# A scan layer with a hand-written slot order: residual products through another PSUM bank, the preparation six slots later

## The chip, the cores and the metric

The kernel runs on one core of one Trainium2 chip. The metric is the device time of one execution in microseconds, as the median of several runs. The core has a TensorE (PE), a VectorE (DVE), a ScalarE (ACT) and a GpSimd (POOL); SyncE (SP) issues most of the transfers. Each engine works off its own list of instructions in order, and waits on semaphores for the others.

## The reference

The input x is 2 sequences of 4096 tokens with 256 features. The first layer is a selective scan (the reference calls it attention), the second a mixture of 16 experts. Each is wrapped in `x + layernorm(layer(layernorm(x)))`. The change touches the first layer only:

```python
xn = _rmsnorm(x, rms_w)
xs, res = jnp.split(xn @ W_in, 2, axis=-1)          # 512 and 512 channels
xs = silu(causal_depthwise_conv(xs, conv_w) + conv_b)
dt, Bm, Cm = split(xs @ W_x)                        # 512, 16, 16
dt = softplus(dt @ W_dt)
A_disc = exp(-exp(A_log) * dt[..., None])
Bx = dt[..., None] * Bm[:, :, None, :] * xs[..., None]
# per channel and state, over the tokens: h = A_disc * h + Bx; y = sum over the 16 states of h * C
y = y * silu(res)
return residual + y @ W_out
```

## The kernel before

**Tiles and steps.** The tokens are cut into 16 tiles of 512, the two sequences in turn. Step i scans tile i. It is divided into 64 slots: slot t holds scan t, which runs 128 of the 8192 pairs of a channel and a state over the 512 tokens of the tile. `all_steps` (L246) writes out the steps; two steps form the body of a hardware loop, the first two and the last ones stand outside. Four scans in a row are a quad, 16 quads a tile.

**What a scan needs.** ACT makes its decay, exp(a * dt), in one of three PSUM banks `pa` (L678), two slots ahead; DVE scans (L822) with the input bq. The input product of a quad (`rep` times `B`) is made for even quads, and for quads 13 and 15, by DVE (L808), for the odd quads 1 to 11 by POOL (L930). After a quad is scanned, ACT saves the carry (L671), POOL multiplies the states by C (L937, "states" below), and PE sums over the states into the bank `py` (L372). DVE multiplies four summed quads by the gate (L828). bq has two buffers, h has four.

**What stands beside it.** Each engine's `step` walks through the slots and calls, at slot t, the preparation `prep` of the next tiles and the work `post` after a tile. The table `PREP` gives for each piece of the preparation its slot, counted from the start of the step before the tile's own: a slot of -19 is slot 45 of two steps before, 84 is slot 20 of the tile's own step. In order: turning the normalised input (PE, with the copy on ACT), then for each of four blocks m of 128 channels the projection (`pe_in`, L391), its copy (`act_in`, L579), the convolution as four matmul taps (`pe_conv`, L399), and its copy with bias (`act_xs`, L586); then one SiLU over the four (`silu_x`, L594), the products for B and C (`pe_bc`, L415; copy L603), the four dt products (`pe_dt`, L425) with the softplus: |x| and exp(-|x|) on ACT (L611, L614), `o1` on DVE (L751), then one Ln (L620), and per group `s` on ACT (L627), `o2`, `o3` on DVE (L756, L760), `u` on POOL (L905). The 16 transfers `rep` (L304) bring dt and u of a group to the layout of the scans. The residual half of the projection, which becomes the gate, is `pe_res` (L406), `act_res` (L591) and, in the tile's own step, `silu_g` (L597).

**Banks.** All eight PSUM banks are in use: three `pa`, two `pb` (for B), `py`, `pp` and `po`. Turns, projections, convolutions, bc, dt and the residual products go one after the other through the single bank `pp`; `USES` lists their order, and each user waits until the reader of the one before has freed it (semaphore `s_free`). `po` takes the output product of `post` (L448), read by DVE for `z` (L783, slots 15 and 22), the transposes and products of the router (L463, L469, L481), whose last reader is the copy of the logits (L667, slot 25), and the softplus terms `s` and `o2`.

**The norm ahead.** `head` normalises tile i+2 in step i: statistics on DVE (slots 30 and 31), scale on ACT (slot 32), a power on POOL (slot 33, L896 and L898), and the application on ACT (L560), at t == 8 of `head`, which is slot 38. POOL has the addition for x1 (L920) at slot 32.

**Before the first step** each engine walks through the slots from `FIRST_SLOT` to 63 for tile 0 (and those below zero for tile 1) with no scans. The last two steps of `all_steps` finish the last tiles, and the experts follow.

Of the kernel before, what the change touches and what calls it, by code (L numbers as in the profile page):

```python
# [11 lines left out]
P = 128  # L12
# [3 lines left out]
DI = 512  # L16
NS = 16
TAPS = 4
KC = DM // P
DC = DI // P  # L20
# [21 lines left out]
    pe_turn=(-22, -20), act_turn=(-21, -19),  # L42
    pe_in=(-19, -13, -7, -1), act_in=(-17, -11, -5, 1), pe_conv=((-16, -15), (-10, -9), (-4, -3), (2, 3)),
    keep_in=(-15, -9, -3, 3), act_xs=(-13, -7, -1, 5), silu_x=5,
    pe_bc=(7, 8), act_bc=10, store_bc=11, load_c=12, load_b=60, sel=(58, 55, 111, 115),
    pe_dt=((11, 12), (17, 18), (22, 23), (36, 37)), abs=(14, 21, 25, 39), exp=(15, 22, 26, 40), o1=(16, 23, 28, 41),
    pe_res=(28, 30, 32, 34), act_res=(30, 32, 34, 36), silu_g=84, keep_r=24,
    ln=42, s=(44, 47, 50, 53), o2=(45, 48, 51, 54), o3=(46, 49, 52, 55), u=(47, 50, 53, 56), rep=(50, 63, 79, 95))
# [20 lines left out]
USES = ([("turn", k) for k in range(KC)] + [(name, m) for m in range(DC) for name in ("in", "xs")] + [("bc", 0)] + [("dt", c) for c in range(3)]  # L69
        + [("res", m) for m in range(DC)] + [("dt", 3)])  # L70
# [62 lines left out]
def scan_layers(nc, sem, TILES, S, ident, mhalf, xf, outf, rms_w, W_in, conv_w, conv_b, W_x, W_dt, A_log, W_out,  # L133
                r_w1, r_w2, hid_dram, acc_dram, lg_dram, bc_dram):

    with ExitStack() as ctx:
# [86 lines left out]
        s_xs, s_sg = sem("xs_ready"), sem("gate_ready")  # L223
        d_bcs, d_crep, d_brep, s_brep = (sem("bc_stored"), sem("c_loaded"), sem("b_loaded"),
# [31 lines left out]
        with nc.Block() as block:  # L256
# [108 lines left out]
            def _(pe):  # L365
# [10 lines left out]
                def prep(t, i, par):  # L376
# [10 lines left out]
                    for m in range(DC):  # L387
# [15 lines left out]
                        if t == PREP["pe_res"][m]:  # L403
                            bank_free("res", m)
                            for k in range(KC):
                                mm = pe.matmul(pp[:], w_in[:, k, DI + m * P:DI + (m + 1) * P], xnt[:, k, :],  # L406
                                               start=(k == 0), stop=(k == KC - 1))
                            mm.then_inc(s_pp, 1)
# [140 lines left out]
            def _(act):  # L549
                def head(t, i):  # L550
# [6 lines left out]
                    if t == 8:  # L557
# [6 lines left out]
                def prep(t, i, par):  # L564
# [8 lines left out]
                    for m in range(DC):  # L573
# [13 lines left out]
                        if t == PREP["act_res"][m]:  # L587
                            full = filled("res", m)
                            if m == 0:
                                atleast(act, s_wo, 2 * (i - 1))  # L590
                            act.copy(gate[:, par, m, :], full).then_inc(s_free, 1)  # L591
# [3 lines left out]
                    if t == PREP["silu_g"]:  # L595
                        act.wait_ge(s_free, NU * i + use("res", DC - 1) + 1)
# [809 lines left out]
```

## Time and profile before

| | us |
|---|---|
| Median of 3 runs | 2389.81 (2388.8 to 2390.92) |
| The profiled execution, its time | 2398.99 |
| The profiled execution, its span | 2397.3 |
| DVE busy | 1902.4 (79%) |
| POOL busy | 1877.0 (78%) |
| PE busy | 1632.2 (68%) |
| ACT busy | 1355.7 (57%) |
| Scans (L822), 1024 of 1266 ns | 1255.3 |
| States products (L937), 256 of 4532 ns | 1158.0 |
| Decays (L678), 1024 of 687 ns | 696.5 |

The profile is of one execution with the profiler on. A busy share is an average over the whole span: the beginning has no scans, and the last 300 us are the experts. In a timeline, instructions of the same kind that follow each other are merged into one row ("x6"), and the bracket at the end gives the idle time of the engine before the row and the instruction that ended it. The instructions of an engine overlap by some 0.1 us, so the distance between the starts of two rows is a little less than the length of the first.

### The profile page before, as it was taken

The page shows a single profiled execution, that of the slowest core. Times are in us where ns is not written, and L with a number is a line of the kernel's source. Part 1 is how long each engine was busy: PE and PEld are TensorE (multiplying, and loading weights), DVE is VectorE, ACT ScalarE, POOL GpSimd, SP SyncE. Part 2 cuts the span into 40 slices and gives each one's busy share as a digit, 9 for nine tenths or more (in the row PEclk, how much of TensorE's full clock was granted, in tenths as well). Part 3 has the DMA queues.
Part 4 walks back from the last instruction along what each step waited for, and adds up shares of the span by engine and source line. Part 5 has one row for each costly group of instructions (what it writes and reads, how often), then busy time and mean ns, then how long its engine had stood idle before and what let it go on. Part 6 is the DMA issues. An engine that isn't in the chain of part 4 may idle for free. (4 is left out here: it accounts for less than half of the span.)

```text
span 2397.3 us, 22571 instructions
## 1 busy us (share of the span) xinstructions
PE 1632.2 (68%) x5460; PEld 625.4 (26%) x5460; DVE 1902.4 (79%) x2195; ACT 1355.7 (57%) x2466; POOL 1877.0 (78%) x634
## 2 busy tenths in 40 slices
PE   6676768686868777776777676877686865340780
PEld 2222223222222222222223232322232211010680
DVE  1169999989899999989898989899899899937012
ACT  2356666666666666676666666666667664530121
POOL 0059898989898988888889888898989898930556
PEclk9888989898988989898888898889798986565895
DMA  2093525253444444443434343535252535203852
GB/s 83 20 257 83 128 62 134 56 129 72 114 91 105 98 106 98 105 89 98 96 86 102 95 99 88 115 83 121 62 134 54 125 68 129 57 28 115 271 146 71
DMA packets 135582, 244.15 MB, mean 102 GB/s; under 512 B 26032, under 2 KB 78010, under 8 KB 135472
## 3 DMA queue, kind: packets, MB, share of 16 engines
q1 hardware_dynamic: 129584, 232.79, 40.0%
q0 software_dynamic: 5888, 10.29, 1.9%
q14 instruction: 90, 0.74, 0.1%
q8 instruction: 20, 0.33, 0.1%
HBM read 77.88 MB, written 31.13 MB: 45 GB/s over the span
## 5 line engine op out<-in xcount | busy, mean ns | idle before, releaser
L822 DVE TENSOR_TENSOR_SCAN h<-pa,carry,bq 128x512 f32<-128x512 f32 x1024 | 1255.3, 1266 | 156.1 <-ACT pa L678 149.0
L937 POOL TENSOR_TENSOR h<-h,c_rep 128x2048 f32<-128x2048 f32 x256 | 1158.0, 4532 | 126.4 <-ACT carry L671 125.7
L678 ACT ACTIVATE pa<-rep,neg_a 128x512 f32<-128x512 f32 x1024 | 696.5, 687 | 407.7 <-DVE h L822 405.0
L930 POOL TENSOR_TENSOR bq<-rep,b_rep 128x2048 f32<-128x2048 f32 x96 | 434.2, 4523 | 87.6 <-DVE h L822 85.4
L372 PE MATMUL py<-h,blk 128*32 128x512 f32 x2048 | 326.0, 701 | 177.8 <-DVE gate L828 127.3
L808 DVE TENSOR_TENSOR bq<-rep,pb 128x2048 f32<-128x2048 f32 x160 | 361.8, 2261 | 9.8 <-PE pb L434 9.8
L425 PE MATMUL pp<-xs,w_dtx 128*128 128x512 f32 x512 | 270.5, 662 | 87.8 <-DVE du L751 76.2
L399 PE MATMUL pp<-xsp,w_conv 128*128 128x512 f32 x512 | 247.7, 614 | 14.2 <-ACT xsp L579 14.2
L391 PE MATMUL pp<-xnt,w_in 128*128 128x512 f32 x256 | 179.7, 840 | 113.9 <-ACT xs L586 92.0
L406 PE MATMUL pp<-xnt,w_in 128*128 128x512 f32 x256 | 143.7, 689 | 73.1 <-DVE du L751 42.7
L425 PEld LDWEIGHTS pp<-xs,w_dtx 128*128 128x128 f32 x512 | 98.1, 205 | 235.7 <-issue 111.4
L372 PEld LDWEIGHTS py<-h,blk 128*32 128x32 f32 x2048 | 44.9, 116 | 390.6 <-issue 176.1
L448 PE MATMUL po<-w_out,gate 128*128 128x256 f32 x512 | 131.1, 392 | 12.7 <-DVE z L783 11.9
L399 PEld LDWEIGHTS pp<-xsp,w_conv 128*128 128x128 f32 x512 | 92.0, 192 | 155.8 <-issue 115.4
L751 DVE SCALAR_TENSOR_TENSOR du<-pp,du 128x512 f32<-128x512 f32 x64 | 43.5, 679 | 104.1 <-ACT du L614 104.0
L415 PE MATMUL pp<-xs,w_bc 128*32 128x512 f32 x128 | 88.1, 853 | 46.2 <-ACT xs L594 46.2
L448 PEld LDWEIGHTS po<-w_out,gate 128*128 128x128 f32 x512 | 96.2, 193 | 78.5 <-issue 41.7
L391 PEld LDWEIGHTS pp<-xnt,w_in 128*128 128x128 f32 x256 | 55.8, 241 | 205.6 <-ACT xs L586 131.7
L896 POOL TENSOR_TENSOR rs<-var,mhalf 128x8 f32<-128x8 f32 x16 | 26.6, 1665 | 97.8 <-ACT var L556 97.8
L905 POOL TENSOR_TENSOR du<-du,xs 128x512 f32<-128x512 f32 x64 | 81.1, 1267 | 23.0 <-DVE du L760 22.9
L611 ACT ACTIVATE du<-pp 128x512 f32<-128x512 f32 x64 | 37.6, 587 | 107.7 <-PE pp L425 107.7
L406 PEld LDWEIGHTS pp<-xnt,w_in 128*128 128x128 f32 x256 | 47.2, 205 | 168.6 <-ACT gate L591 66.0
(159 smaller groups left out, 1756.4 us busy)
## 6 DMA issues: line engine op xcount, KB each, us to landing
rep<-du SPq DMA_DIRECT2D x1024, 128.0 KB, 2.4
c_rep<-bc_scratch SPq DMA_DIRECT2D x64, 256.0 KB, 5.1
combine_scratch<-zeros SPq DMA_DIRECT2D x16, 520.0 KB, 7.3
xt<-in_L_attn_x_dram SPq DMA_DIRECT2D x16, 512.0 KB, 3.4
b_rep<-bc_scratch SPq DMA_DIRECT2D x64, 128.0 KB, 3.5
xo<-in_L_attn_x_dram SPq DMA_DIRECT2D x16, 512.0 KB, 3.6
out_dram<-z SPq DMA_DIRECT2D x16, 512.0 KB, 3.0
hidden_scratch<-late SPq DMA_DIRECT2D x16, 512.0 KB, 3.1
```

The source lines that it names most:

```text
L372: mm = pe.matmul(py[32 * j:32 * j + 32, :], blk[:], h[:, quad % 4, j, :], start=(g == 0), stop=(g == 3), tile_position=(0, 32 * j))
L391: mm = pe.matmul(pp[:], w_in[:, k, m * P:(m + 1) * P], xnt[:, k, :], start=(k == 0), stop=(k == KC - 1))
L399: mm = pe.matmul(pp[:], w_conv[:, m, tap, :], xsp[:, m % 2, tap:tap + T], start=(tap == 0), stop=(tap == TAPS - 1))
L406: mm = pe.matmul(pp[:], w_in[:, k, DI + m * P:DI + (m + 1) * P], xnt[:, k, :], start=(k == 0), stop=(k == KC - 1))
L415: mm = pe.matmul(pp[32 * par:32 * par + 32, :], w_bc[:, k, :], xs[:, k, :], start=(k == 0), stop=(k == DC - 1), tile_position=(0, 32 * par))
L425: mm = pe.matmul(pp[:], w_dtx[:, k, c * P:(c + 1) * P], xs[:, k, :], start=(k == 0), stop=(k == DC - 1))
L448: mm = pe.matmul(po[:, (s % 2) * DM:(s % 2 + 1) * DM], gate[:, par, k, s * P:(s + 1) * P], w_out[:, k, :], start=(k == 0), stop=(k == DC - 1))
L678: act.activation(pa[:, decay_bank(t), :], rep[:, c % 2, t % 4, 0, :], ACT.Exp, scale=neg_a[:, a_column(t):a_column(t) + 1]).then_inc(s_exp, 1)
L808: v.tensor_tensor(bq[:, quad % 2], rep[:, c % 2, :, 1, :], pb[:, pb_bank, :].unsqueeze(1).broadcast_to((P, 4, T)), ALU.mult).then_inc(s_bd, 1)
L822: v.tensor_tensor_scan(h[:, quad % 4, t % 4, :], pa[:, decay_bank(t), :], bq[:, quad % 2, t % 4, :], carry[:, par, t:t + 1], ALU.mult, ALU ...
L930: pool.tensor_tensor(bq[:, 1], rep[:, c % 2, :, 1, :], b_rep[:, g // 2, :].unsqueeze(1).broadcast_to((P, 4, T)), ALU.mult).then_inc(s_bp, 1)
L937: pool.tensor_tensor(h[:, quad % 4], h[:, quad % 4], c_rep[:, par, quad % 4, :].unsqueeze(1).broadcast_to((P, 4, T)), ALU.mult).then_inc(s ...
```

## The change

The residual products are written to `po` instead of `pp` and leave the list `USES`. They have semaphores of their own: `s_res` (product done), `s_rese` (copied to the gate). The first of a tile waits until `po` has been read by `z` and by the copy of the logits; each further one waits for the copy of the one before. The preparation from the turns to the last o1 is some six slots later: the turns at 48 and 50 of the step before instead of 42 and 44, the fourth block at slots 5 to 11 instead of -1 to 5. SiLU stands two slots behind the last copy instead of in its slot (13 instead of 5), the dt products at 18 to 38, Ln at 44 instead of 42, s, o2, o3 and u one to three slots later, rep 0 at 52 instead of 50. The norm is applied at t == 11 of `head`, slot 41. No instruction is added or left out.

```diff
--- before.py
+++ after.py
@@ -39,13 +39,13 @@
 
 
 PREP = dict(
-    pe_turn=(-22, -20), act_turn=(-21, -19),
-    pe_in=(-19, -13, -7, -1), act_in=(-17, -11, -5, 1), pe_conv=((-16, -15), (-10, -9), (-4, -3), (2, 3)),
-    keep_in=(-15, -9, -3, 3), act_xs=(-13, -7, -1, 5), silu_x=5,
-    pe_bc=(7, 8), act_bc=10, store_bc=11, load_c=12, load_b=60, sel=(58, 55, 111, 115),
-    pe_dt=((11, 12), (17, 18), (22, 23), (36, 37)), abs=(14, 21, 25, 39), exp=(15, 22, 26, 40), o1=(16, 23, 28, 41),
-    pe_res=(28, 30, 32, 34), act_res=(30, 32, 34, 36), silu_g=84, keep_r=24,
-    ln=42, s=(44, 47, 50, 53), o2=(45, 48, 51, 54), o3=(46, 49, 52, 55), u=(47, 50, 53, 56), rep=(50, 63, 79, 95))
+    pe_turn=(-16, -14), act_turn=(-15, -13),
+    pe_in=(-13, -7, -1, 5), act_in=(-11, -5, 1, 7), pe_conv=((-10, -9), (-4, -3), (2, 3), (8, 9)),
+    keep_in=(-9, -3, 3, 9), act_xs=(-7, -1, 5, 11), silu_x=13,
+    pe_bc=(14, 15), act_bc=17, store_bc=18, load_c=19, load_b=60, sel=(58, 55, 111, 115),
+    pe_dt=((18, 19), (24, 25), (31, 32), (37, 38)), abs=(21, 28, 34, 40), exp=(22, 29, 35, 41), o1=(23, 30, 36, 42),
+    pe_res=(27, 30, 33, 36), act_res=(29, 32, 35, 38), silu_g=84, keep_r=24,
+    ln=44, s=(46, 49, 52, 55), o2=(47, 50, 53, 56), o3=(48, 51, 54, 57), u=(49, 52, 55, 58), rep=(52, 63, 79, 95))
 FIRST_SLOT = PREP["pe_turn"][0]
 
 
@@ -66,8 +66,8 @@
 SPREADS = ((0, 0, 0, 15), (2, 1, 2, 14), (1, 0, 13, 12), (3, 0, 15, 13))
 
 
-USES = ([("turn", k) for k in range(KC)] + [(name, m) for m in range(DC) for name in ("in", "xs")] + [("bc", 0)] + [("dt", c) for c in range(3)]
-        + [("res", m) for m in range(DC)] + [("dt", 3)])
+USES = ([("turn", k) for k in range(KC)] + [(name, m) for m in range(DC) for name in ("in", "xs")] + [("bc", 0)]
+        + [("dt", c) for c in range(DC)])
 NU = len(USES)
 
 
@@ -221,6 +221,7 @@
         s_r1, s_halo = sem("r1_kept"), sem("halo_kept")
         s_pp, s_free = sem("prep_bank_full"), sem("prep_bank_free")
         s_xs, s_sg = sem("xs_ready"), sem("gate_ready")
+        s_res, s_rese = sem("residual_product"), sem("residual_copied")
         d_bcs, d_crep, d_brep, s_brep = (sem("bc_stored"), sem("c_loaded"), sem("b_loaded"),
                                          [sem(f"b_spread_{n}") for n in range(len(SPREADS))])
         s_abs, s_sp, s_o1, s_ln, s_s, s_o2 = (sem("softplus_abs"), sem("softplus_exp"), sem("softplus_head"),
@@ -401,11 +402,15 @@
                                 if n == 1:
                                     mm.then_inc(s_pp, 1)
                         if t == PREP["pe_res"][m]:
-                            bank_free("res", m)
+                            if m == 0:
+                                atleast(pe, s_z, 2 * (i - 1))
+                                atleast(pe, s_lg, i - 2)
+                            else:
+                                pe.wait_ge(s_rese, DC * i + m)
                             for k in range(KC):
-                                mm = pe.matmul(pp[:], w_in[:, k, DI + m * P:DI + (m + 1) * P], xnt[:, k, :],
+                                mm = pe.matmul(po[:], w_in[:, k, DI + m * P:DI + (m + 1) * P], xnt[:, k, :],
                                                start=(k == 0), stop=(k == KC - 1))
-                            mm.then_inc(s_pp, 1)
+                            mm.then_inc(s_res, 1)
                     for n, at in enumerate(PREP["pe_bc"]):
                         if t == at:
                             if n == 0:
@@ -554,7 +559,7 @@
                         act.activation(mean[:], mv[:, :, 0], ACT.Identity, scale=-1.0)
                         act.activation(var[:, 0:SUB], mv[:, :, 1], ACT.Identity, bias=eps[:, 0:1])
                         act.activation(var[:, SUB:], mv[:, :, 1], ACT.Identity, scale=1.0 + EPS, bias=eps[:, 1:2]).then_inc(s_st, 1)
-                    if t == 8:
+                    if t == 11:
                         act.wait_ge(s_nm, i + 1)
                         for s in range(SUB):
                             ins = act.activation(xt[:, s, :], xt[:, s, :], ACT.Identity, scale=rs[:, SUB + s:SUB + s + 1],
@@ -585,15 +590,15 @@
                             atleast(act, s_u, DC * (i - 1) + m + 1)
                             act.activation(xs[:, m, :], full, ACT.Identity, bias=cb[:, m:m + 1]).then_inc(s_free, 1)
                         if t == PREP["act_res"][m]:
-                            full = filled("res", m)
+                            act.wait_ge(s_res, DC * i + m + 1)
                             if m == 0:
                                 atleast(act, s_wo, 2 * (i - 1))
-                            act.copy(gate[:, par, m, :], full).then_inc(s_free, 1)
+                            act.copy(gate[:, par, m, :], po[:]).then_inc(s_rese, 1)
                     if t == PREP["silu_x"]:
                         act.wait_ge(s_free, NU * i + use("xs", DC - 1) + 1)
                         act.activation(xs[:], xs[:], ACT.Silu).then_inc(s_xs, 1)
                     if t == PREP["silu_g"]:
-                        act.wait_ge(s_free, NU * i + use("res", DC - 1) + 1)
+                        act.wait_ge(s_rese, DC * i + DC)
                         act.activation(gate[:, par], gate[:, par], ACT.Silu).then_inc(s_sg, 1)
                     if t == PREP["act_bc"]:
                         act.wait_ge(s_pp, NU * i + use("bc") + 1)
```

## Rows read from the trace of the kernel before

**Rows 1.** Table of stretches: the middle 1750 us; engines' busy time, clock, DMA share

```profile
200.00:1950.00 1750.00, 1300.04 (x4106) 453.32 (x4106) 1598.38 (x1689) 1141.56 (x2081) 1547.41 (x460) 0.87 0.42 97
```

**Rows 2.** Waits from 200 to 1950: total us, times, longest

```profile
DVE h L822 <- ACT pa L678: 136.8, 57, 4.4
DVE du L751 <- ACT du L614: 11.1, 27, 0.5
```

**Rows 3.** Timeline of DVE, one step: start, length, instruction, idle before it

```profile
1014.47 2.46 DVE L822 TENSOR_TENSOR_SCAN h<-pa,carry,bq 128x512 f32<-128x512 f32 x2 [2.02 <-ACT pa L678]
...
1025.68 2.46 DVE L822 TENSOR_TENSOR_SCAN h<-pa,carry,bq 128x512 f32<-128x512 f32 x2 [4.21 <-ACT pa L678]
...
1037.90 0.85 DVE L783 SCALAR_TENSOR_TENSOR z<-xo,r,po 128x256 f32<-128x256 f32 x2
...
1061.40 1.28 DVE L822 TENSOR_TENSOR_SCAN h<-pa,carry,bq 128x512 f32<-128x512 f32 x1 [1.49 <-ACT pa L678]
...
1070.53 7.13 DVE L822 TENSOR_TENSOR_SCAN h<-pa,carry,bq 128x512 f32<-128x512 f32 x6
1077.57 2.26 DVE L808 TENSOR_TENSOR bq<-rep,pb 128x2048 f32<-128x2048 f32 x1
1079.75 3.63 DVE L822 TENSOR_TENSOR_SCAN h<-pa,carry,bq 128x512 f32<-128x512 f32 x3
1086.32 1.28 DVE L822 TENSOR_TENSOR_SCAN h<-pa,carry,bq 128x512 f32<-128x512 f32 x1 [2.94 <-ACT pa L678]
...
1093.24 2.53 DVE L822 TENSOR_TENSOR_SCAN h<-pa,carry,bq 128x512 f32<-128x512 f32 x2
```

**Rows 4.** Timeline of ACT in the same step

```profile
1019.56 0.69 ACT L586 ACTIVATE xs<-pp,cb 128x512 f32<-128x512 f32 x1 [3.08 <-PE pp L399]
1020.27 1.28 ACT L594 ACT_TABLE_LOAD   x1
1021.56 1.91 ACT L594 ACTIVATE xs<-xs 128x2048 f32<-128x2048 f32 x1
...
1059.58 0.60 ACT L611 ACTIVATE du<-pp 128x512 f32<-128x512 f32 x1 [4.64 <-PE pp L425]
...
1083.64 2.07 ACT L560 ACTIVATE xt<-xt,nm,rs 128x256 f32<-128x256 f32 x4 [5.23 <-POOL nm L898]
```

**Rows 5.** Timeline of PE in the same step

```profile
1009.13 3.06 PE L391 MATMUL pp<-xnt,w_in 128*128 128x512 f32 x4 [2.48 <-ACT xs L586]
...
1017.64 1.88 PE L399 MATMUL pp<-xsp,w_conv 128*128 128x512 f32 x4
...
1097.64 3.78 PE L391 MATMUL pp<-xnt,w_in 128*128 128x512 f32 x4 [1.50 <-ACT xnt L572]
```

**Rows 6.** Timeline of POOL in the same step

```profile
1070.39 4.53 POOL L930 TENSOR_TENSOR bq<-rep,b_rep 128x2048 f32<-128x2048 f32 x1 [2.41 <-DVE h L822]
...
1092.51 9.03 POOL L937 TENSOR_TENSOR h<-h,c_rep 128x2048 f32<-128x2048 f32 x2
```

**Rows 7.** Table of stretches; the third number from the end is the granted clock

```profile
1030.00:1049.00 19.00, 17.47 (x72) 9.04 (x71) 19.00 (x17) 12.34 (x19) 17.38 (x5) 1.00 0.81 169
...
1091.00:1101.30 10.30, 6.17 (x16) 2.60 (x12) 10.30 (x16) 8.35 (x14) 10.30 (x3) 0.50 0.00 0
```

**Rows 8.** Timelines of DVE and of POOL, the last step with a preparation

```profile
1967.02 2.46 DVE L822 TENSOR_TENSOR_SCAN h<-pa,carry,bq 128x512 f32<-128x512 f32 x2 [1.23 <-ACT pa L678]
...
1962.41 4.52 POOL L930 TENSOR_TENSOR bq<-rep,b_rep 128x2048 f32<-128x2048 f32 x1
```

**Rows 9.** Timelines of PE, ACT and DVE before the first scan

```profile
95.61 1.98 PE L406 MATMUL pp<-xnt,w_in 128*128 128x512 f32 x4 [2.07 <-DVE du L751]
...
111.26 1.28 ACT L620 ACT_TABLE_LOAD   x1
...
143.25 0.69 ACT L586 ACTIVATE xs<-pp,cb 128x512 f32<-128x512 f32 x1 [3.78 <-PE pp L399]
...
145.98 7.16 DVE L822 TENSOR_TENSOR_SCAN h<-pa,carry,bq 128x512 f32<-128x512 f32 x6 [3.97 <-ACT pa L678]
```

## The prediction, made before the kernel ran

> **What bounds the kernel now.** I read the page first: DVE is busy for 79% of the span, POOL for 78%, and the chain that ended last covers only the expert stage, so it says nothing of the scan layer. That layer runs from about 140 to 2060 us and consists of 16 steps, one per tile. In its middle DVE is busy for 1598 of 1750 us and POOL for 1547 [rows 1]; per step (125.3 us on average, from the 14 steps of that stretch) that is 114 and 111 us. So DVE sets the pace, and its idle time, 10.9 us a step, is all there is to win without taking work off it. The list of waits names nearly all of it: scans waiting for a decay bank from ACT, 136.8 us in 57 waits, and the softplus head o1 waiting for ACT, 11.1 us in 27 [rows 2]. It also shows why ACT was late: it stood waiting for PE and, once a step, for POOL.
>
> The timeline of one step gives each stall its slot (I count scans to find the slot) [rows 3]: 2.02 us before scan 4, 4.21 before scan 8, 1.49 before scan 28, 2.94 before scan 41, 10.7 us together; the two waits of an o1 a step, 0.4 each [rows 2], come to it. Their causes are on ACT [rows 4]. Slot 5: it waits 3.08 us for the last convolution, then does two table loads and a SiLU, 4.5 us. Slot 25: it waits 4.64 us for the third dt product, whose start by the code stands behind o1 of slot 23. Slot 38: it waits 5.23 us for the norm's scale, which POOL gives late. POOL's own rows [rows 6] show the point on which my forecast rests: from the end of scan 31 (1070.25) POOL works without a gap: input product 9, states 7, the x1 addition, the power, states 8, input product 11, until 1092.5; scan 44, which reads the last, starts at 1093.24.
>
> **Lengths.** A scan advances DVE by 1.19 us (six in 7.13), an input product by 2.18 (1077.57 to 1079.75), a half of z by 0.8. From 1061.40 to 1070.53 lie four scans, an input product, one o1 and one set of stats and aggregate: 2.2 us for the last two. From 1086.32 to 1093.24 lie three scans, a wait of 0.4, and the same two with a gate product: 2.9, so a gate product is 0.6 to 0.7; o1 is as short as it (0.6), stats and aggregate 1.6 [rows 3]. On POOL a states product takes 4.5, an input product 4.5 [rows 6].
>
> **Part by part, slots 57 to 5.** All moves by six slots, and the blocks of the projection are six slots apart, so slots 57 to 5 hold the same pattern one block earlier (act_xs at 63, act_in at 1, conv at 2 and 3, act_xs at 5). The stall before scan 4 stays as it is. I take nothing there.
>
> **Slots 5 to 12.** The SiLU leaves slot 5, and the fourth block comes in: projection at 5, copy at 7, convolution at 8 and 9, copy at 11. With the SiLU gone ACT has the decay of scan 8 ready at 1020.9 against 1021.5 wanted: the 4.21 us go. The new chain: copy of slot 5 ends 1020.2, projection 2.0 us warm or 3.1 as in 1009.13 [rows 5], copy to about 1023.0, decay of scan 10 usable at 1023.8 to 1024.9; DVE wants it at 1024.4, after two scans and the gate product. The sum of quad 15, which the gate product needs, now stands behind the projection on PE and ends at 1023.4 to 1025. Cost 0 to 1.5, taken 0.1, since PE comes from the convolution of 1017.64, which ran at 1.88 us for four matmuls [rows 5], after a gap of only 0.9.
>
> **Slots 13 to 23.** SiLU at 13: from the end of scan 12 ACT needs decay 0.8 + 4.5 + 0.9 until scan 16 can start = 6.2; DVE has scan 13, input product 4, scans 14 and 15, half z: 6.5. Covered, as long as ACT is on time; uncovered it costs up to 4.5, as at slot 5. I take 0.1. POOL: from the end of scan 7, input product 3, states 1 and 2, input product 5 take 18.1, and DVE arrives at scan 20 after 17.9: 0.2. PE waits for this SiLU at slot 14 with bc (8 matmuls), then two out pieces, a sum, dt 0, two out pieces and half of z behind it: 3.7 + 1.9 + 1.0 + 3.7 + 1.9 = 12.2 us at the 1.88 per four matmuls that [rows 5] show, from 1032.9 to 1045.1, where z of slot 22 wants it at 1045.4. Cost 0 to 2, taken 0.2. o1 of slot 23 waits 0.4 as o1 of 23 does now.
>
> **Slots 24 to 31.** dt 1 starts after o1 at 23 and is due at 28, five slots on; in the kernel before dt 2 had two slots. The 1.49 goes. The residual products wait no longer for the pp bank but for po: for the logits copy at 25 and for each other. They cost PE the same and lie in its free time. One o1 (0.6 us) leaves this stretch for slot 36.
> Sum from the end of scan 7 (1025.68 - 4.21 = 1021.47) to the end of scan 31 (1070.25, just before POOL's 1070.39): now 48.8. After: 24 scans 28.5, three input products 6.5, two gates 1.2, z 1.6, two o1 1.2, stats twice 2.9 (one aggregate falls after scan 31) = 41.9, plus 0.9 of the stalls above = 42.8. Gain 6.0.
>
> **Slots 32 to 44.** The norm moves from 38 to 41, so ACT no longer waits for POOL: 2.94 and the 0.4 of the last o1 go by their names. But the POOL chain after scan 31 (22.2 us, then the scan) does not get shorter, and DVE's own work there is 8.1 + 2.2 + 3.6 + 6.4 = 20.4 us (an o1 more than before at 36). So scan 44 waits about 2.1 us for input product 11, and the stretch goes from 23.0 to 22.4: gain 0.6, not 3.4. The same binding is in the trace already where no norm is in the way: in the step that begins near 1885 product 11 ends at 1966.9 and scan 44 starts at 1967.02, 1.23 late [rows 8]. (The profile puts that wait down to ACT; ACT's decay for it was long done.) The Ln at 44 hides behind that same wait.
>
> **Slots 45 to 56.** Turns, s, o2, o3 two to six slots later, order kept. The u products move from 47 to 49 and so behind states 11 in POOL's queue (4.5 us), and the 16 copies of rep 0 behind them (10 us of issue and 2.4 to landing). They would land some 7 us before input product 0 of slot 61 wants them: 0. SP: store_bc and load_c now queue behind rep 2 of slot 15, c_rep is wanted only in the next step: 0.
>
> A full step thus gains 6.6; there are 13 with everything in them: 86. I take 84, as the stalls of single steps vary by some tenths. The first step has no x1 addition and ends POOL-bound: about 4; the last with a preparation has no norm: 5.
>
> **Before the first scan.** The order written out there now ends with one projection block of tile 1 less. With the residual products off the pp bank, dt 2 and 3 no longer stand behind four of them with their copies (the first begins at 95.61, 2.07 us after the work before it [rows 9], and each of the others waits for a copy). Four of them with their copies took 10.6 us, of which only the half that PE itself needs remains on the chain (5.3); the chain from the Ln to the last act_xs then holds one block of projection, convolution and copy less (7.4 us from act_xs to act_xs), and about 1 more for the turns, which now stand behind the first s and o3. So the Ln's table load starts at 106 instead of 111.3, and the last act_xs before the decays ends at 132 instead of 143.9 [rows 9]. The first scan: about 134.5 instead of 146. Gain 11.5; at least the 5 of the Ln, at most 14.
>
> Sum: 84 + 4 + 5 + 11.5 = 104.5. On the span of 2397.3 (time of that execution 2399.0) this gives 2293; on the median of 2389.8, which lies 9 us below that execution, it gives **2285**; I carry the saving over as it is.
>
> **A rule against this.** [Rows 4] show a table load of 1.28 and the SiLU 1.29 after its start, so a switch costs 1.29. The Trainium skill, "ScalarE: Activation LUTs", section "What ACT_TABLE_LOAD costs", adds about 1.38 us of drain to each switch. By that the SiLU of slot 13 would hold ACT 2.8 longer and stall each of 15 steps by 2.5 to 2.8, an estimate from the page of about 2324; the trace contradicts it.
>
> **Rivals.** (1) The tight places of slots 5 to 22 give way: cold projection 1.0 to 1.5, z late 1 to 2, SiLU uncovered by as much. For: my slack there is 0.3 us in three places. Against: PE worked at the full level over just such a stretch [rows 7], and the SiLU's cover is counted in whole instructions of fixed length. Two such stalls of 1.3 take 2.6 from 6.6 in 15 steps: 2285 + 39 = 2324. (2) The SiLU's stall moves rather than goes: 4.2 us, as now at scan 8. It would need ACT to reach slot 13 more than 4 us late. 2285 + 15 x 4.2 = 2348. (3) Slower: PE's queue between the SiLU and z at the 1.2 GHz level. Four matmuls that take 1.98 took 3.78 at 1097.64, at a granted clock of 0.50 [rows 5, 7]. The 12.2 us would be 24.4, z of slot 22 12 us late, each step 5.5 us worse than now: 2285 + 15 x 12 = 2465. It turns from a gain to a loss when that queue takes over 19.1 us. Against: the granted clock was 1.00 from 1030 to 1049 [rows 7], and PE has fewer gaps now. (4) The POOL bound is not there: DVE gets product 11 in time, because POOL overlaps more than its rows show; then slots 32 to 44 gain 2.1 more: 2285 - 14 x 2.1 = 2256. (5) No change: everything won before scan 31 is lost at scan 44. That would need POOL's chain from scan 7 on to take 71 us; its rows add up to 64.2.
>
> **Chances.** Forecast 0.60, (1) 0.20, (2) 0.06, (3) 0.04, (4) 0.06, (5) 0.04. The forecast's own spread is 2272 to 2300: prologue 5 to 14, a step 5.8 to 7.2. The range takes in rival (1): 2268 to 2326. Faster by over 0.2% (what a measurement of this kernel can tell) 0.92, within 0.2% 0.03, slower 0.05.
>
> **What would show it.** Step length 118.7 instead of 125.3; no stall before scans 8, 28 and 41; a new one of about 2 us before scan 44 that ends with POOL's input product 11; the one before scan 4 unchanged; scan 0 at 134 to 136; L560 on ACT without a wait. Wrong would be: PE's copy wait at slot 11 over 2 us, z late at slot 22, or ACT idle for POOL anywhere between slots 25 and 41.

## The result and the profile after

The changed kernel takes 2287.19 us (median; 2283.65 to 2290.35), the kernel before 2390.07 in the same session: a ratio of 0.957 (95% interval 0.9553 to 0.9586), 102.9 us less. The forecast was 2285.

| | before | after |
|---|---|---|
| The profiled execution, its span | 2397.3 | 2287.4 |
| DVE busy | 1902.4 (79%) | 1896.8 (83%) |
| POOL busy | 1877.0 (78%) | 1875.7 (82%) |
| Scan 0 starts at | 145.98 | 136.66 |
| From scan 0 to scan 44, first step | 76.07 | 72.29 |
| From scan 44 of the first step to scan 12 of the last | 1803.14 | 1714.78 |
| What remains | 372.1 | 363.7 |

The scan layer is 101.5 us shorter: 9.3 before the first scan, 3.8 in the first step, 88.4 in the steps between. What remains has the same instructions and differs by 8.4 us all the same; about as much (9 us) as the profiled execution of before lay above its median. Three of the runs below keep before's instructions there too, and their profiles give 364.1, 363.1 and 364.2 us for the same stretch. So the 8.4 us belong to that one execution of before and not to the change. The lines that follow answer to [rows 1] (table of stretches, the same 1750 us) and [rows 2] (waits of DVE in them).

```profile
200.00:1950.00 1750.00, 1321.23 (x4259) 466.25 (x4261) 1678.23 (x1772) 1195.10 (x2162) 1629.20 (x482) 0.86 0.43 101
...
DVE h L827 <- POOL bq L935: 36.9, 26, 2.3
DVE h L827 <- ACT pa L683: 30.2, 22, 2.8
...
DVE du L756 <- ACT du L619: 0.8, 2, 0.5
```

DVE stands still for 72 of 1750 us instead of 152. The scans' waits for ACT fell from 136.8 to 30.2 us, and a name that the list did not have before is now first: scans waiting for POOL's input product, 36.9 us. One step of DVE, against [rows 3]:

```profile
845.52 5.02 DVE L827 TENSOR_TENSOR_SCAN h<-pa,carry,bq 128x512 f32<-128x512 f32 x4 [1.72 <-ACT pa L683]
...
852.64 4.80 DVE L827 TENSOR_TENSOR_SCAN h<-pa,carry,bq 128x512 f32<-128x512 f32 x4
857.36 0.67 DVE L833 TENSOR_TENSOR gate<-py,gate 128x512 f32<-128x512 f32 x1
...
873.34 2.46 DVE L827 TENSOR_TENSOR_SCAN h<-pa,carry,bq 128x512 f32<-128x512 f32 x2 [0.57 <-POOL bq L935]
...
879.09 0.85 DVE L788 SCALAR_TENSOR_TENSOR z<-xo,r,po 128x256 f32<-128x256 f32 x2
...
896.37 1.27 DVE L827 TENSOR_TENSOR_SCAN h<-pa,carry,bq 128x512 f32<-128x512 f32 x1
...
919.94 2.46 DVE L827 TENSOR_TENSOR_SCAN h<-pa,carry,bq 128x512 f32<-128x512 f32 x2 [2.32 <-POOL bq L935]
```

The rows are scans 2 to 5 (this one follows the loop's edge; in the step after it the wait is before scan 4, 0.68), 6 to 9, the gate, scans 20 and 21, half of z, scan 31, and scans 44 and 45. The stalls before scans 8, 28 and 41 are gone; two waits for POOL have come. On average over the 13 steps behind the first, DVE's scans wait 1.7 us before scans 2 and 4 together (1.4 in the kernel before), 0.7 before scan 20 and 2.3 before scan 44. On POOL, against [rows 6], the chain that ends at scan 44:

```profile
897.72 4.54 POOL L935 TENSOR_TENSOR bq<-rep,b_rep 128x2048 f32<-128x2048 f32 x1 [0.82 <-DVE h L827]
902.21 4.55 POOL L942 TENSOR_TENSOR h<-h,c_rep 128x2048 f32<-128x2048 f32 x1
906.69 2.39 POOL L925 TENSOR_TENSOR z<-z,xo 128x1024 f32<-128x1024 f32 x1
909.01 1.68 POOL L901 TENSOR_TENSOR rs<-var,mhalf 128x8 f32<-128x8 f32 x1
...
910.92 4.52 POOL L942 TENSOR_TENSOR h<-h,c_rep 128x2048 f32<-128x2048 f32 x1
915.39 4.52 POOL L935 TENSOR_TENSOR bq<-rep,b_rep 128x2048 f32<-128x2048 f32 x1
```

Nothing idles in it from 897.72 to 919.91, and scan 44 starts at 919.94. On ACT, against [rows 4]: the copy of slot 11, the SiLU of slot 13 with its two table loads and the decays behind it, and the norm, which waits for nobody now.

```profile
860.34 0.69 ACT L591 ACTIVATE xs<-pp,cb 128x512 f32<-128x512 f32 x1 [0.39 <-PE pp L400]
...
862.33 1.28 ACT L599 ACT_TABLE_LOAD   x1
863.63 1.91 ACT L599 ACTIVATE xs<-xs 128x2048 f32<-128x2048 f32 x1
865.56 1.28 ACT L683 ACT_TABLE_LOAD   x1
866.86 1.91 ACT L683 ACTIVATE pa<-rep,neg_a 128x512 f32<-128x512 f32 x3
...
912.50 2.06 ACT L565 ACTIVATE xt<-xt,nm,rs 128x256 f32<-128x256 f32 x4
```

### The profile page after: what moved, and what is told of

Read it like the earlier page. It is cut to its first block and busy times, and to the rows that moved or that the text cites. A ratio compares the mean times of both kernels' runs of the same rounds, so it can differ in the third digit from the quotient of the medians.

```text
span 2287.4 us, 22530 instructions
## 1 busy us (share of the span) xinstructions
PE 1597.8 (70%) x5460; PEld 620.7 (27%) x5460; DVE 1896.8 (83%) x2195; ACT 1357.9 (59%) x2466; POOL 1875.7 (82%) x634
## 5 line engine op out<-in xcount | busy, mean ns | idle before, releaser
L827 DVE TENSOR_TENSOR_SCAN h<-pa,carry,bq 128x512 f32<-128x512 f32 x1024 | 1250.9, 1266 | 80.2 <-POOL bq L935 36.9
L373 PE MATMUL py<-h,blk 128*32 128x512 f32 x2048 | 338.2, 735 | 325.9 <-POOL h L942 268.4
L400 PE MATMUL pp<-xsp,w_conv 128*128 128x512 f32 x512 | 261.4, 642 | 12.9 <-ACT xsp L584 12.9
L430 PE MATMUL pp<-xs,w_dtx 128*128 128x512 f32 x512 | 246.7, 621 | 30.4 <-DVE du L756 29.6
L392 PE MATMUL pp<-xnt,w_in 128*128 128x512 f32 x256 | 164.6, 777 | 81.3 <-ACT xs L591 68.2
L430 PEld LDWEIGHTS pp<-xs,w_dtx 128*128 128x128 f32 x512 | 94.7, 196 | 181.6 <-issue 117.6
L411 PE MATMUL po<-xnt,w_in 128*128 128x512 f32 x256 | 129.6, 630 | 12.4 <-ACT gate L596 11.2
L453 PE MATMUL po<-w_out,gate 128*128 128x256 f32 x512 | 124.2, 392 | 4.1 <-DVE z L788 3.3
L439 PE MATMUL pb<-bc,sel_b 32*128 32x512 f32 x128 | 100.1, 872 | 14.3 <-DVE bq L813 14.3
L392 PEld LDWEIGHTS pp<-xnt,w_in 128*128 128x128 f32 x256 | 53.4, 231 | 180.7 <-ACT xs L591 107.9
L1199 DVE TENSOR_TENSOR act<-act,pv 128x512 f32<-128x512 f32 x16 | 11.0, 688 | 84.3 <-PE pv L1316 84.3
L591 ACT ACTIVATE xs<-pp,cb 128x512 f32<-128x512 f32 x64 | 43.4, 679 | 56.9 <-PE pp L400 56.8
```

Of the source, the lines that this page charges most:

```text
L373: mm = pe.matmul(py[32 * j:32 * j + 32, :], blk[:], h[:, quad % 4, j, :], start=(g == 0), stop=(g == 3), tile_position=(0, 32 * j))
L392: mm = pe.matmul(pp[:], w_in[:, k, m * P:(m + 1) * P], xnt[:, k, :], start=(k == 0), stop=(k == KC - 1))
L400: mm = pe.matmul(pp[:], w_conv[:, m, tap, :], xsp[:, m % 2, tap:tap + T], start=(tap == 0), stop=(tap == TAPS - 1))
L411: mm = pe.matmul(po[:], w_in[:, k, DI + m * P:DI + (m + 1) * P], xnt[:, k, :], start=(k == 0), stop=(k == KC - 1))
L430: mm = pe.matmul(pp[:], w_dtx[:, k, c * P:(c + 1) * P], xs[:, k, :], start=(k == 0), stop=(k == DC - 1))
L439: pe.matmul(pb[:, bank, :], sel_b[b:b + 32, g, :], bc[b:b + 32, :], start=True, stop=True, tile_position=(b, 0)).then_inc(s_brep[n], 1)
```

## The experiments

Two theories go into them. Mine: ACT's stalls are won up to scan 31, of which the SiLU is most; from scan 31 to 44 POOL's chain sets the time, so the norm is worth little. The rival: ACT bounds all along, each stall named for ACT is worth its length, and the wait before scan 44 is a leftover of the same kind. Line numbers of experiments that start from the kernel before with the new bank are those of after. Each ratio is to executions of the kernel before that ran beside the experiment (medians of 2389.7 to 2391.4), while 2287.19 comes from the first session. A few us more or less than after are therefore not shown by the times alone, and there I go by the steps in the profiles, which in two kernels with the same slots (before and the bank alone) add up to the same 1803.14 us. An average step is from scan 44 to scan 44, over the 13 steps behind the first.

### The bank alone

The kernel before with the residual products in `po`, at before's slots.

```diff
-USES = (... + [("dt", c) for c in range(3)] + [("res", m) for m in range(DC)] + [("dt", 3)])
+USES = (... + [("dt", c) for c in range(DC)])
...
-                                mm = pe.matmul(pp[:], w_in[:, k, DI + m * P:DI + (m + 1) * P], xnt[:, k, :],
+                                mm = pe.matmul(po[:], w_in[:, k, DI + m * P:DI + (m + 1) * P], xnt[:, k, :],
```

> The slots of the kernel before, with the residual products through po and out of the list of the pp bank (nothing else changed). Theory of the prediction: the stalls of a step come from the slots of SiLU, of the third dt product and of the norm, not from the bank; the step stays at 125.3 us, and only the stretch before the first scan gains about 2 us: 2388 (2382 to 2392). Rival: the freed pp bank is what lets the dt chain run ahead and brings a good part of the 103 us: 2355 or less, with the stall before scan 28 gone.

Measured: 2386.63, ratio 0.9981 (0.9971 to 0.9991) to 2391.01. The stalls of a step stand as they were:

```profile
771.83 2.46 DVE L827 TENSOR_TENSOR_SCAN h<-pa,carry,bq 128x512 f32<-128x512 f32 x2 [3.93 <-ACT pa L683]
...
807.83 1.28 DVE L827 TENSOR_TENSOR_SCAN h<-pa,carry,bq 128x512 f32<-128x512 f32 x1 [1.58 <-ACT pa L683]
...
832.74 1.28 DVE L827 TENSOR_TENSOR_SCAN h<-pa,carry,bq 128x512 f32<-128x512 f32 x1 [2.59 <-ACT pa L683]
```

Scan 0 starts at 143.62 instead of 145.98, and from scan 44 of the first step to scan 12 of the last it is 1803.14 us in both kernels. So the new bank alone brings 4 us, of which the profile shows some 2 before the first scan and none in the steps; the rest I cannot place. The other 99 come from the slots, some of which need the bank.

### The norm at its old slot, and at its new slot in the kernel before

```diff
-                    if t == 11:
+                    if t == 8:
                         act.wait_ge(s_nm, i + 1)
```

> The changed kernel with the norm applied at slot 38 again instead of 41. Theory: from the end of scan 31 POOL's chain needs 22.2 us to input product 11 wherever the norm stands, so the stall before scan 41 comes back (about 2.9 us) and the one before scan 44 (2.3) goes; the sum is 23.0 against 22.4, with an o1 more than before perhaps 23.3: 0.6 to 0.9 a step in 13 steps, 8 to 12 us: 2297 (2293 to 2303). Rival: the stalls add up, as their names say: 13 x 3.4 = 44: 2331.

Measured: 2290.83, ratio 0.9585 (0.9569 to 0.9601), 3.6 us above after, with intervals that overlap. Scans 41, 44 and 47 of one step, and POOL's input product 11:

```profile
912.49 1.28 DVE L827 TENSOR_TENSOR_SCAN h<-pa,carry,bq 128x512 f32<-128x512 f32 x1 [2.36 <-ACT pa L683]
...
918.84 2.42 DVE L827 TENSOR_TENSOR_SCAN h<-pa,carry,bq 128x512 f32<-128x512 f32 x2
...
925.02 1.28 DVE L827 TENSOR_TENSOR_SCAN h<-pa,carry,bq 128x512 f32<-128x512 f32 x1 [0.38 <-ACT pa L683]
...
914.19 4.52 POOL L935 TENSOR_TENSOR bq<-rep,b_rep 128x2048 f32<-128x2048 f32 x1
```

With the stall before scan 41 back, the wait before scan 44 is gone: 2.4 us of idle time stand under ACT's name in one kernel and under POOL's in the other. Product 11 ends at 918.71, just before DVE reaches scan 44 at 918.84, and from the end of scan 31 to scan 44 it is 22.4 us on average against 22.3 in after. A step is 0.5 us longer nearly all the same (118.9 against 118.5), and the only new wait is the 0.38 before scan 47.

My 2297 was too high for two reasons. An o1 (0.6 us) now stands ahead of the stall and shortens it from 2.94 to 2.36, and the last o1 no longer waits 0.4 us behind it, so the stretch is 22.4 and not 23.0 to 23.3 us. And the move has a second effect, which neither theory had: before the first scan, where the order is the same but nothing is scanned, the norm of tile 1 now stands ahead of the last softplus group and not between it and the Ln, which brings 1.7 us (its rows are shown further down, under "Before the first scan"). So the run is 5.9 us slower in the steps (to scan 12 of the last) and 3.3 us earlier at scan 0. The reverse, the kernel before with t == 11 (`-if t == 8:` `+if t == 11:`):

> The kernel before with the norm applied at slot 41 instead of 38, nothing else. Theory: the stall of 2.9 before scan 41 turns into one of about 2.3 before scan 44: gain 0.6 a step in 13 steps, 8 us: 2382 (2377 to 2387). Rival: the norm's move is worth its stall of 2.9 to 3.4: 2348.

Measured: 2382.89, ratio 0.9968 (0.9958 to 0.9979), 8 us faster, of which the profile has 6.9 in the steps. The stall moved to scan 44 and changed its name, at nearly its size:

```profile
1092.39 2.46 DVE L822 TENSOR_TENSOR_SCAN h<-pa,carry,bq 128x512 f32<-128x512 f32 x2 [2.89 <-POOL bq L930]
```

The rival's 2.9 to 3.4 a step would have been some 42 us.

### The third dt product alone

From the kernel with the bank alone:

```diff
-    pe_dt=((11, 12), (17, 18), (22, 23), (36, 37)), abs=(14, 21, 25, 39), exp=(15, 22, 26, 40), o1=(16, 23, 28, 41),
+    pe_dt=((11, 12), (17, 18), (24, 25), (36, 37)), abs=(14, 21, 28, 39), exp=(15, 22, 29, 40), o1=(16, 23, 30, 41),
```

> As the run with the slots of before and the residual products through po (2386.6), and only the third dt product moved from slots 22 and 23 to 24 and 25, its |x| from 25 to 28, exp to 29, o1 to 30, which the order of the pp bank did not allow before. Theory: the stall of 1.5 before scan 28 goes; POOL's chain, which is late after scan 31 anyway, takes none of it back, as input product 9 waits for scan 31: 15 x 1.4 = 21: 2366 (2362 to 2371). Rival: POOL or the norm's wait takes it back: 2385.

Measured: 2367.36, ratio 0.9887 (0.9849 to 0.9924), 19.3 us below the bank alone, or 1.3 a step. The 1.5 before scan 28 is gone and the other two stalls stay (3.93 and 2.59 in the step that I read). So this term of the sum was real. By the code it needs the bank, since with the residual products in `pp` the first of them, at slot 28, would wait for the o1 at 30; that was not tried.

### The SiLU two slots earlier

```diff
-    keep_in=(-9, -3, 3, 9), act_xs=(-7, -1, 5, 11), silu_x=13,
+    keep_in=(-9, -3, 3, 9), act_xs=(-7, -1, 5, 11), silu_x=11,
```

> The changed kernel with SiLU in the slot of the last convolution copy (11) instead of two slots behind it. Theory: ACT is then held from about 6.2 us after the end of scan 7 for 4.5 us, so scan 14 can start 1.7 us after DVE wants it (it comes after input product 4, 2.2 us of cover instead of 5.3): 1.5 to 2 a step in 15 steps, less what POOL's bound at scan 20 (0.56) gives back: 17 to 26 us: 2308 (2302 to 2314). Rival (what counts is that SiLU left the wrap of the step, its slot within 11 to 13 is of no matter): 2287 to 2290.

Measured: 2308.8, ratio 0.9648 (0.9613 to 0.9684), 21.6 us above after. Size as expected, way not quite. DVE at scans 14 and 20, then POOL:

```profile
873.58 2.46 DVE L827 TENSOR_TENSOR_SCAN h<-pa,carry,bq 128x512 f32<-128x512 f32 x2 [1.38 <-ACT pa L683]
...
882.88 2.46 DVE L827 TENSOR_TENSOR_SCAN h<-pa,carry,bq 128x512 f32<-128x512 f32 x2 [1.35 <-POOL bq L935]
...
873.74 4.52 POOL L942 TENSOR_TENSOR h<-h,c_rep 128x2048 f32<-128x2048 f32 x1 [2.24 <-ACT carry L676]
878.22 4.53 POOL L935 TENSOR_TENSOR bq<-rep,b_rep 128x2048 f32<-128x2048 f32 x1
```

I had written that POOL's wait would give back what the SiLU costs. It does not: the carry of a quad is saved by ACT behind this SiLU, POOL's states product waits 2.24 us for the carry, the input product stands behind it, and scan 20 waits 1.35 instead of 0.57. So the SiLU costs twice, once on DVE and once through POOL. The 1.38 stands before scan 14 in every second step, with 0.69 in most of the others. On average the waits before scans 14 and 20 are 1.0 and 1.3 us instead of 0 and 0.7, those before scans 2 and 4 are 0.5 shorter, and two slots are worth 1.3 us a step.

### The front of the preparation at its old slots

```diff
-    pe_turn=(-16, -14), act_turn=(-15, -13),
-    pe_in=(-13, -7, -1, 5), act_in=(-11, -5, 1, 7), pe_conv=((-10, -9), (-4, -3), (2, 3), (8, 9)),
-    keep_in=(-9, -3, 3, 9), act_xs=(-7, -1, 5, 11), silu_x=13,
+    pe_turn=(-22, -20), act_turn=(-21, -19),
+    pe_in=(-19, -13, -7, -1), act_in=(-17, -11, -5, 1), pe_conv=((-16, -15), (-10, -9), (-4, -3), (2, 3)),
+    keep_in=(-15, -9, -3, 3), act_xs=(-13, -7, -1, 5), silu_x=13,
```

> The changed kernel with the turns, projections, convolutions and their copies in the slots of before (fourth block at -1 to 5), SiLU and all behind it as changed. Theory: the SiLU's move to 13 carries the gain, the six slots of the front carry none in a step, but the stretch before the first scan is one block longer (8 us), and the turns at slot 42 meet the last o1 in the pp bank there (0 to 1.5 a step): 2287 + 8 + 7 = 2302 (2293 to 2316). Rival: the front's shift is needed for the gain of a step: over 2330.

Measured: 2310.53, ratio 0.9657 (0.9621 to 0.9693), 23.3 us above after, the upper part of what I expected. Scan 0 starts 4.8 us later (141.44), and a step is 1.0 us longer at one place, the input product behind scan 49. ACT, PE and DVE there:

```profile
930.75 1.28 ACT L625 ACT_TABLE_LOAD   x1
...
936.18 0.58 ACT L577 COPY xnt<-pp 128x512 f32<-128x512 f32 x1
...
936.81 3.63 PE L392 MATMUL pp<-xnt,w_in 128*128 128x512 f32 x4 [6.07 <-ACT xnt L577]
941.37 1.12 PE L439 MATMUL pb<-bc,sel_b 32*128 32x512 f32 x2
...
942.53 2.29 DVE L813 TENSOR_TENSOR bq<-rep,pb 128x2048 f32<-128x2048 f32 x1 [0.98 <-PE pb L439]
```

The Ln at slot 44 with its two table loads (930.75 to 935.5) now stands ahead of the copy of the second turn, at slot 45. PE idles 6.07 us for that copy where [rows 5] show 1.50, runs the projection at 3.6 us for four matmuls, and behind it stands the spread of B that the input product needs. So the front of the preparation and the Ln had to move together: I had priced moving the front at nothing, which holds only because it keeps clear of the Ln.

### The x1 addition out of POOL's chain

```diff
-    load=-13, ..., stats=(24, 42), pow=(27, 45), z2=30, x1=32,
-    store_x1=35, ...
+    load=-13, ..., stats=(24, 48), pow=(27, 51), z2=30, x1=41,
+    store_x1=45, ...
```

> The changed kernel with the x1 addition on POOL at slot 41 (behind input product 11 and states 9) instead of 32, its statistics at 48, the power at 51, the store at 45. Theory: POOL's chain from scan 31 to input product 11 is 2.3 us shorter, the stall of 2.3 before scan 44 goes to 0.2: 14 steps x 2.1 = 29: 2258 (2254 to 2266). Rival: the wait before scan 44 only has POOL's name and is set by something else (ACT's decay, the o1): no change, 2287.

Measured: 2278.74, ratio 0.9538 (0.9522 to 0.9554), 8.5 us below after where I expected 29. The addition (2.39 us) had left POOL's chain, and yet scan 44 waits:

```profile
1011.95 5.96 DVE L827 TENSOR_TENSOR_SCAN h<-pa,carry,bq 128x512 f32<-128x512 f32 x5
...
1031.68 2.46 DVE L827 TENSOR_TENSOR_SCAN h<-pa,carry,bq 128x512 f32<-128x512 f32 x2 [1.56 <-POOL bq L935]
...
1040.95 1.40 DVE L770 BATCH_NORM_STATS2 st<-z 128x6 f32<-128x256 f32 x4
```

The first row starts with scan 32, the second with scan 44. From the end of scan 31 to scan 44 the stretch fell from 22.4 to 20.0 us, by POOL's 2.4. But x1's statistics had to follow it from slot 42 to 48, and with their aggregates they are 1.65 us of DVE's own work (L770 and L776; their start at 1040.95 is the last row). They stood in the shadow of the wait and now stand behind it, where each costs its length: 2.4 less 1.65 leaves 0.75 a step, and the average step is 117.6 instead of 118.5. Neither theory had it; I had counted POOL's chain and not what DVE does while it waits.

### The power behind product 11

POOL's power for the norm ahead goes from slot 33 to 40, called after the input product of the slot and before the states; ACT applies the norm at slot 46. DVE's order stays.

```diff
-                    if t == 11:
+                    if t == 16:
                         act.wait_ge(s_nm, i + 1)
...
                 def head(t, i):
-                    if t == 3:
+                    if t == 10:
                         pool.wait_ge(s_st, 3 * i + 3)
...
                             inputs(t // 4 + 1, i)
+                        if has_second:
+                            head(t - HEAD_AT, i + 2)
```

> The changed kernel with the norm's power on POOL directly behind input product 11 (slot 40) instead of slot 33, and the norm applied at 46. Here no work of DVE moves with it. Theory: POOL's chain from scan 31 to input product 11 is 1.85 us shorter and nothing is put behind scan 44 on DVE: the wait of 2.3 before scan 44 shrinks to 0.5, 13 steps x 1.8 = 23: 2264 (2258 to 2270). Rival: as with the x1 addition, the time comes back elsewhere (the norm late for the turns, the Ln's 4.5 us no longer under cover at slot 44): 2280.

Measured: 2261.32, ratio 0.9456 (0.9426 to 0.9486), 26 us below after. POOL, then DVE at scan 44:

```profile
896.72 4.51 POOL L942 TENSOR_TENSOR h<-h,c_rep 128x2048 f32<-128x2048 f32 x1
901.19 4.51 POOL L935 TENSOR_TENSOR bq<-rep,b_rep 128x2048 f32<-128x2048 f32 x1
905.67 1.64 POOL L901 TENSOR_TENSOR rs<-var,mhalf 128x8 f32<-128x8 f32 x1
...
905.74 2.46 DVE L827 TENSOR_TENSOR_SCAN h<-pa,carry,bq 128x512 f32<-128x512 f32 x2 [0.41 <-POOL bq L935]
```

Only the 1.85 us of the power and its small product left POOL's chain; the wait fell from 2.32 to 0.41 and the average step from 118.5 to 116.7. In the profile 24.2 us are won from scan 44 of the first step to scan 12 of the last and 1.8 in the first step. Scan 0 stands 2.6 us earlier too, and some 1.7 of that are the edit's: as in the run with the norm at slot 38, the norm of tile 1 no longer stands between the last exp(-|x|) and the Ln before the first scan, here because it now comes behind the Ln. This shows POOL's chain as the bound of the changed kernel there, and the run is faster than both kernels.

### The copy at the start of the step

At the start of a step a stall is left under ACT's name, before scan 2 or 4: 1.7 us a step on average, before scan 4 alone anything from 0.1 to 2.8. The third block's copy and convolution one slot later shorten it:

```diff
-    pe_in=(-13, -7, -1, 5), act_in=(-11, -5, 1, 7), pe_conv=((-10, -9), (-4, -3), (2, 3), (8, 9)),
-    keep_in=(-9, -3, 3, 9), ...
+    pe_in=(-13, -7, -1, 5), act_in=(-11, -5, 2, 7), pe_conv=((-10, -9), (-4, -3), (3, 4), (8, 9)),
+    keep_in=(-9, -3, 4, 9), ...
```

> The changed kernel with the copy of the third projection block at slot 2 instead of 1 (its convolution at 3 and 4, keep_in at 4), so that ACT makes the decay of scan 4 before it waits for PE. Theory: the stall before scan 4 (0.7 to 2.3 a step) shrinks by about 1, but from the end of scan 63 POOL works without a gap (input product 1, states 15 and 0, input product 3, states 1 and 2, input product 5: 31.5 us to scan 20), so the waits before scans 12 and 20 grow by as much: 2287 (2280 to 2289). Rival: the stalls of ACT at the start of a step are worth their length: 14 x 1 = 14: 2273 or less.

Measured: 2282.21, ratio 0.9545 (0.9516 to 0.9574), 5 us below after, with intervals that overlap. In the profile 4.2 us are an earlier scan 0. The SiLU of tile 0 is 3.2 us ahead: 1.7 of it comes before anything differs (eight convolution matmuls near 21 us take 3.67 us instead of 5.47), the rest from the edit itself, which changes the order of the copies before the first scan. DVE's waits from 300 to 1700, first after, then this kernel:

```profile
DVE h L827 <- POOL bq L935: 33.5, 24, 2.3
DVE h L827 <- ACT pa L683: 20.6, 14, 2.8
```

```profile
DVE h L827 <- POOL bq L935: 38.0, 28, 2.3
DVE h L827 <- ACT pa L683: 16.3, 14, 2.2
```

4.3 us went from ACT's line, 4.5 came to POOL's. On average of a step the waits before scans 2 and 4 fall from 1.7 to 1.3 us, those before scans 12 and 20 rise from 0.8 to 1.1. The same edit on top of the power behind product 11:

> As the run with the power behind input product 11 (2261.3), with the copy at slot 2 as in the run before this one. Theory: nothing further, 2261 (2255 to 2264). Rival: 2247.

Measured: 2260.58, ratio 0.9452 (0.9425 to 0.9479), against 0.9456 without it: no difference. Here the waits before scans 2 and 4 fall from 1.4 to 1.2 us a step, those before scans 12 and 20 rise from 0.95 to 1.15, and all waits of the scans are 2.8 us a step in both. So what the edit took from the stall at the start of the step came back as POOL's next waits. It took only a part; that the rest of the stall is worth nothing either is not shown.

## Why the prediction was right, point by point

**Slots 57 to 5.** Taken as unchanged. The waits before scans 2 and 4 average 1.4 us a step before and 1.7 after, so 0.3 a step was missed here; in the last two runs 0.5 and 0.2 us less of it shortened the waits of a step by only 0.1 and by nothing.

**Scan 8 and the projection.** The gate follows scan 9 at once (857.36), the copies of slots 7 and 11 wait 0.39 us for PE; 0.1 was forecast and nothing is seen on DVE.

**SiLU.** Six slots of cover by 6.2 against 6.5 us. No wait to speak of follows the SiLU (0.02 us a step before scan 16, where rival (2) would have had 4.2); the run with two slots less shows that the slack was small, as I had worked out: 1.7 us late was expected before scan 14, and 1.38 or 0.69 came. ACT's rows give 4.53 us from the first load to the first decay behind it. The Trainium skill, "ScalarE: Activation LUTs", section "What ACT_TABLE_LOAD costs", would add about 1.38 us of drain to each of the two switches, 7.2 us in all, an estimate by its figures; the trace does not agree, as the starts at 862.33, 863.63, 865.56 and 866.86 leave no room for it.

**POOL before scan 20.** 0.2 forecast, 0.57 measured in the step shown and 0.66 on average, with 0.11 before scan 12 besides, which I had not forecast. The step was right, the size not: POOL's chain from the end of scan 7 to input product 5 lies that little behind DVE.

**PE's queue to z.** bc at 865.69 to the last out piece at 877.57 is 11.9 us against 12.2, at a granted clock of 1.00:

```profile
865.00:880.00 15.00, 13.64 (x57) 5.52 (x49) 14.43 (x15) 13.49 (x19) 15.00 (x4) 1.00 0.83 189
```

z of slot 22 waits for nothing, nor does the o1 behind it, for which I had taken 0.4 (all waits of an o1 fell from 11.1 to 0.8 us in 1750). Rivals (1) and (3) had their place here, and neither came.

**To scan 31.** From the end of scan 7 (855.02) to the end of scan 31 (897.55) 42.5 us, 42.7 on average; forecast 42.8, before 48.8. The stalls that I listed for it add up to 1.0, not 0.9; those that came, to 0.8.

**To scan 44.** 22.4 us, forecast 22.4, before 23.0. This was the step on which the forecast stood against the list of waits, which offered 2.94 under ACT's name. The two norm experiments settle it: with the norm at 38 and at 41 the stretch is 22.9 and 22.3 us long in the kernel before, 22.4 and 22.3 in the one after, whatever the stall is called. With 1.85 us of POOL's work taken out it is 20.4. Rival (4) falls with them. By my own sum DVE's work there is 20.3 and not 20.4 us, and 20.1 came; so the wait before scan 44 was 2.3 instead of 2.1 at the same length of the stretch.

**The steps.** Scans 44 of four steps stand at 801.47, 919.94, 1038.04 and 1156.94: 118.5 a step, forecast 118.7, so rival (5) is out too. From the first scan 44 to scan 12 of the last step the gain is 88.4 against 89. The first step gained 3.8 against 4. That the layer ends at about 2060 us was misread: the last scan of before ends at 2115. The sum does not use it.

**Before the first scan.** 9.3 gained against 11.5. From the SiLU of tile 0 (its table load at 64.65 before and 66.62 after, in front of which nothing differs) to scan 0 it is 81.3 and 70.0 us, that is 11.3: the number was right, and the execution stood 2 us late at that SiLU. PE after, against [rows 9]:

```profile
87.57 1.88 PE L411 MATMUL po<-xnt,w_in 128*128 128x512 f32 x4
90.12 1.98 PE L411 MATMUL po<-xnt,w_in 128*128 128x512 f32 x4 [0.68 <-ACT gate L596]
91.94 3.60 PE L430 MATMUL pp<-xs,w_dtx 128*128 128x512 f32 x8
95.38 1.88 PE L411 MATMUL po<-xnt,w_in 128*128 128x512 f32 x4
```

The residual products now fill PE between the dt products, and the Ln's table load starts at 106.62 against 106 forecast. My working had missed that in the written-out order an exp(-|x|) stands behind the first residual copy on ACT; it costs ACT 1.1 us, which PE's queue covers. It had also missed what the norm's new slot does there, so that the number is right partly by luck. ACT in after, then in the run with the norm at slot 38:

```profile
104.55 2.06 ACT L565 ACTIVATE xt<-xt,nm,rs 128x256 f32<-128x256 f32 x4
106.62 1.28 ACT L625 ACT_TABLE_LOAD   x1
```

```profile
101.17 2.07 ACT L565 ACTIVATE xt<-xt,nm,rs 128x256 f32<-128x256 f32 x4
105.40 1.28 ACT L625 ACT_TABLE_LOAD   x1
```

In after the norm of tile 1 holds up the Ln by most of its length, while in the other run ACT applies it when it would wait for PE. There the Ln comes 1.7 us earlier, counted from the SiLU of tile 0, and scan 0 3.8 us earlier. Most of the rest is PE's clock: the first convolution behind the Ln takes 3.78 us for four matmuls in after (119.37, at a granted clock of 0.50) and 1.99 in the other run (118.16, at 1.00). That part I do not put down to the norm: in the last run above the norm is out of the Ln's way too, and that convolution takes 3.78 us all the same.

**What stays open.** Some 2 of the 4 us of the bank alone are not to be found in the profiles. Why the waits before scans 2 and 4 grew by 0.3 us a step no run isolates. Nor does one show why PE's clock rose earlier before the first scan in two of the runs.

## What to carry to other kernels

A stall's name is the engine that came last, not what the time would be without it: between two fixed points, add up the work of each engine that the second one waits for, and forecast the longest of the sums. Here 2.9 us under ACT's name were worth 0.6, as POOL's chain ended less than 1 us before the same point. To shorten such a stretch take work out of the engine whose chain is longest (1.85 us of POOL brought 1.8 a step), and do not move the waiting engine's own work past the waiting point, since it was free only in front of it. A slot that is moved for the steps also moves in the stretch before the first scan, where nothing covers it: look at both (1.7 us here).

## What the runs showed of the hardware

Four matmuls of 128x512 took 1.88 to 1.98 us on a PE that came from work, at a granted clock of 1.00 (87 to 98 us in after), that is 2.4 GHz. They took 3.63 us after 6.07 us of idle time in the run with the front at its old slots, at a granted clock of 0.53 over these 3.6 us, for the most part 1.2 GHz. The two levels stand in [rows 5] and [rows 7] already; what I had not expected is that the slow one reaches DVE through two small matmuls (1.12 us) that spread B, only because they are queued behind the slow ones. At 1.9 us the projection would, by an estimate from these rows, have let them end before DVE wanted them; no run tried it. And nothing in the profile names that cause: DVE's row says `PE pb`, and only PE's own rows show that it had been idle and then slow.
